# Dense layers of a two-layer graph network, chunk by chunk with nodes on partitions

## What is computed

```python
def block(x):                                  # N = 3125, D = 128, H = 4, C = 32, HID = 512
    conv = transformer_conv(x, src, dst, ...)  # softmax over incoming edges, + x @ Wskip.T + bskip
    out1 = conv @ Wout.T + bout
    out2 = _layer_norm(out1 + x, ln1_w, ln1_b)
    h = jax.nn.relu(out2 @ W1.T + b1)
    out3 = h @ W2.T + b2
    return _layer_norm(out3 + out2, ln2_w, ln2_b)
x = _layernorm(x + block(x))
# second layer: w = mlp(embedding(edge_weight)); rows of x @ W_up gathered by src, multiplied by w
# and the edge's direction, summed by dst, then @ W_out
x = _layernorm(x + edge_conv(x, edge_attr_3, edge_weight, src, dst, ...))
return x
```

## Time and profile before

| | us |
|---|---|
| median of 3 runs (2353.87 to 2362.63) | 2357.6 |
| the profiled execution | 2362.86 |
| its span, first to last instruction | 2361.1 |
| first edge loop and its tail end at | 1124.7 |
| dense layers, to the first gather of the second loop | 1299.7 |
| second edge loop ends at | 2321.7 |

### The profile page before, as it was taken

How to read it: one execution, slowest core, us unless ns; L and a number is a source line. 1 busy time by engine, 2 the same in 40 slices (tenths; PEclk the granted TensorE clock), 3 DMA queues, 4 the chain that set the end, 5 groups by cost and what they waited for, 6 DMA issues and landing times.

```text
span 2361.1 us, 43013 instructions
## 1 busy us (share of the span) xinstructions
PE 1914.8 (81%) x12714; PEld 1563.0 (66%) x12714; DVE 1643.9 (70%) x4394; ACT 1201.3 (51%) x2979; POOL 1563.6 (66%) x1617
## 2 busy tenths in 40 slices
PE   5567767776777677676998999989899898998988
PEld 4567667766677667676637666666667676766666
DVE  4767767777767767678413677777777777777774
ACT  2656556565656556552233454445545455454551
POOL 4777777777777777770000777777777777777770
PEclk8799998999989989989797799999999999999997
DMA  8656556555555555560000222222222222222221
GB/s 262 167 155 169 164 152 167 165 162 164 161 167 166 164 159 164 152 180 14 1 0 27 57 57 57 56 57 56 58 57 57 57 57 56 57 57 56 57 55 35
DMA packets 209005, 240.86 MB, mean 102 GB/s; under 512 B 43003, under 2 KB 166268, under 8 KB 208518
## 3 DMA queue, kind: packets, MB, share of 16 engines
q0 software_dynamic: 64480, 158.57, 25.1%
q1 hardware_dynamic: 144294, 79.55, 11.7%
HBM read 226.01 MB, written 11.94 MB: 101 GB/s over the span
## 4 chain that ended last, share of the span: by engine, by line
POOL 54%; issue 20%; PE 15%; DVE 4%; ACT 3%; DMA 3%; DVEq 0%; SPq 0%; POOLq 0%; ACTq 0%
POOL rows L397 32%; POOL rows L384 22%; PE ps L448 3%; PE ps L439 2%; PE ps L550 2%; DVE acc L912 2%; DMA rows<-kv_tab,src_col 2%; PE ps L430 1%; ACT hots L654 1%; PE ps L541 1%; PE ps L571 1%; PE ps L532 1%; PE ps L566 1%; ACT exb L677 1%; ACT hots L657 1%
## 5 line engine op out<-in xcount | busy, mean ns | idle before, releaser
L397 POOL DMA_INDIRECT rows<-up_tab,src_col x806 | 764.0, 948 | 390.2 <-issue 245.3
L384 POOL DMA_INDIRECT rows<-kv_tab,src_col x806 | 793.8, 985 | 272.8 <-issue 266.8
L620 PE MATMUL ps<-hotT,hots 128*128 128x128 f32 x3232 | 453.1, 298 | 87.2 <-DVE hots L1125 87.0
L620 PEld LDWEIGHTS ps<-hotT,hots 128*128 128x128 f32 x3232 | 412.5, 207 | 122.0 <-DVE hots L1125 114.2
L912 DVE TENSOR_TENSOR acc<-acc,ps 128x256 f32 x808 | 335.9, 416 | 216.9 <-PE ps L448 192.2
L1089 DVE TENSOR_TENSOR acc<-acc,ps 128x256 f32 x808 | 334.4, 414 | 15.0 <-PE ps L620 13.1
L448 PE MATMUL ps<-hots,msg 128*128 128x128 f32 x1616 | 329.1, 287 | 9.8 <-DVE acc L912 7.3
L448 PE MATMUL ps<-hots,exb 128*128 128x128 f32 x1616 | 322.1, 282 | 0.0
L668 ACT COPY hotT<-ps 128x512 f32<-128x512 f32 x202 | 117.8, 583 | 359.6 <-PE ps L430 347.9
L1104 DVE TENSOR_TENSOR hots<-rows,yvec 128x384 f32<-128x384 f32 x202 | 114.1, 565 | 235.8 <-DMA rows<-up_tab,src_col 235.8
L448 PEld LDWEIGHTS ps<-hots,msg 128*128 128x128 f32 x1616 | 260.4, 203 | 13.7 <-issue 7.5
(11 more groups left out here) (142 smaller groups left out, 2518.2 us busy)
## 6 DMA issues: line engine op xcount, KB each, us to landing
qwin<-q_tab SPq DMA_DIRECT2D x808, 64.0 KB
rows<-kv_tab,src_col POOLq DMA_INDIRECT x806, 2.9
rows<-up_tab,src_col POOLq DMA_INDIRECT x806, 2.5
hots<-emb_rows SPq DMA_DIRECT2D x202, 16.0 KB
weights<-r_far SPq DMA_DIRECT2D x25, 128.0 KB, 3.5
emb_rows<-weights SPq DMA_DIRECT2D x25, 128.0 KB
kv_tab<-rows SPq DMA_DIRECT2D x12, 256.0 KB, 2.8
dst_lanes<-in_dst_lanes SPq DMA_DIRECT2D x26, 65.0 KB
```

The costliest lines, as they stand in the source:

```text
L384: nc.gpsimd.indirect_dma_start(kvr[:, q % RING, k, :], None, kv_tab, bass.IndirectOffsetOnAxis(src_col[:, t:t + 1].bitcast(U32), 0)).then_ ...
L397: nc.gpsimd.indirect_dma_start(upr[:, q % RING, k, :], None, up_tab, bass.IndirectOffsetOnAxis(src_col[:, t:t + 1].bitcast(U32), 0)).then_ ...
L620: mm = pe.matmul(ps[:, 4 + 2 * (q % 2) + k // 2, (2 * (k % 2) + m) * P:(2 * (k % 2) + m + 1) * P], left[:, q % 2, k, :], hot2[:, q % 2, k, ...
```

## The change

Stage 3 becomes one loop over the chunks in which each engine's list interleaves steps of chunks j-1, j, j+1 and j+2. Up to the division features stay on partitions; the output projection takes a tile's columns as stationary operand and so gives nodes on partitions (`first_out`, into PSUM bank 2). A node's mean and variance are then taken along the row by DVE (`bn_stats`, `bn_aggr` in `moments_of`); ACT takes the root and applies mean and scale in one pass per tile (`normalise`). `turn1` transposes to features for the hidden layer, where `second_input` applies the first norm's weight and bias; `mlp` gives rows again, with the residual as a product with the identity. `centre` and `third_input` apply the second norm together with x and its bias row; `turn2` transposes the third norm's input ahead of that norm, whose mean is folded into `wup` and whose scale is applied in `up_rows`. The new x is written later by `new_x`.

The skip layer is folded: `wx` = Wskip.T Wout.T + I and the row `const1` = bskip Wout.T + bout. `prepare` makes them in the tail of the first edge loop: a transpose in PE's slot 203 and three products in slot 205; a copy and two scalings on DVE at the end of slot 204 and four 128x128 operations in slot 206. SP loads x by rows (`x_rows`, 1.6 MB) after `msg_ready` 190 and four vectors over all partitions. POOL adds the second norm's bias row to `xb` after the last gather of the first loop and ahead of the memset of `acc`. The final stage has nodes on partitions too, with two buffers `last`, and stores rows of the result. Left out below: the views into SBUF, the semaphores, functions that a sentence above describes, and all removed lines; `kv_in` and `g_in` become one list `rows_in`.

```diff
             batch_rows(BATCHES - 1)
+            sp.wait_ge(msg_ready, 190)
+            sp.dma_start(xb.rearrange("p t f -> p (t f)"), a["x_rows"]).then_inc(ld["dense"], 16)
+            sp.wait_ge(qe_ready, 200)
+            sp.dma_start(qwin[:, 3].rearrange("p t f -> p (t f)"), a["row_vecs"].partition_broadcast(P)).then_inc(ld["dense"], 16)
...
+                sp.wait_ge(fin_ready, j + 1)
+                tiles = chunk_tiles(j)
+                full = [t for t in tiles if (t + 1) * P <= N]
+                if full:
+                    sp.dma_start(out[full[0] * P:(full[-1] + 1) * P, :].rearrange("(t p) f -> p t f", p=P),
+                                 last[:, j % 2, 0:len(full), :]).then_inc(fin_out, 16)
...
+            pool.wait_ge(ld["dense"], 32)
+            nc.gpsimd.tensor_tensor(xb, xb, row_l2b.unsqueeze(1).to_broadcast([P, TABLE_TILES, D]), ALU.add).then_inc(xb_ready, 1)
             pool.wait_ge(conv, NCH)
             nc.gpsimd.memset(acc[:], 0.0).then_inc(acc2_zero, 1)
...
+                if q in (NQ + 1, NQ + 3):
+                    prepare((q - NQ) // 2)
...
+            def first_out(j):
+                pe.wait_ge(conv, j + 1)
+                if j:
+                    pe.wait_ge(u1_sb, j)
+                for k, t in enumerate(chunk_tiles(j)):
+                    to = ps[:, 2, k * P:(k + 1) * P]
+                    pe.matmul(to, xT[:, tile_cols(t)], wx, start=True, stop=False)
+                    mm = pe.matmul(to, convs[:, j % 2, k * P:(k + 1) * P], wt(W_OUT), start=False, stop=True)
+                mm.then_inc(out1_mm, 1)
...
+                    pe.wait_ge(out2_sb, j)
+                for k in range(count(j)):
...
+            def mlp(j, ks):
+                pe.wait_ge(h_sb, 4 * (j + 1))
+                if j:
+                    pe.wait_ge(u2_sb, j)
+                for k in ks:
+                    to = ps[:, 6, k * P:(k + 1) * P]
+                    pe.matmul(to, out2T[:, j % 2, k * P:(k + 1) * P], ident, start=True, stop=False)
+                    for m in range(HID // P):
+                        mm = pe.matmul(to, hiddens[:, j % 2, m, k * P:(k + 1) * P], wt(W_2 + m * P), start=False, stop=(m == HID // P - 1))
+                if ks and ks[-1] == count(j) - 1:
+                    mm.then_inc(mlp_mm, 1)
...
+            denominators(0)
+            inverses(0)
+            denominators(1)
+            first_out(0)
+            turn1(0)
+            for j in range(NCH + 1):
+                ks = list(range(count(j))) if j < NCH else []
+                if j + 1 < NCH:
+                    inverses(j + 1)
                 if j < NCH:
+                    hidden(j, 0)
+                    hidden(j, 1)
+                if j + 1 < NCH:
+                    first_out(j + 1)
+                if j < NCH:
+                    hidden(j, 2)
+                    hidden(j, 3)
+                if j + 2 < NCH:
+                    denominators(j + 2)
+                if j:
+                    turn2(j - 1)
+                if j < NCH:
+                    mlp(j, ks[:2])
+                if j:
+                    up(j - 1)
+                if j < NCH and ks[2:]:
+                    mlp(j, ks[2:])
+                if j + 1 < NCH:
+                    turn1(j + 1)
             pe.wait_ge(up_sb, NCH)
...
+            def root(n, j):
+                act.wait_ge(moment[n], j + 1)
+                nc.scalar.activation(rstd[:, n, j % 2, 0:count(j)], moments[:, n, j % 2, 0:count(j), 1], ACT.Sqrt,
+                                     bias=consts[:, K_EPS:K_EPS + 1]).then_inc(std[n], 1)
+            def normalise(n, j, to, ready):
+                act.wait_ge(shift[n], j + 1)
+                for k in range(count(j)):
+                    op = nc.scalar.activation(to(k), to(k), ACT.Identity, bias=nshift[:, n, j % 2, k:k + 1], scale=rstd[:, n, j % 2, k:k + 1])
+                op.then_inc(ready, 1)
...
+            spread_inverse(1)
+            first_normal(0)
+            for j in range(NCH + 1):
+                if j < NCH:
+                    second_input(j)
+                    relu(j, 0)
+                    relu(j, 1)
+                if j:
+                    root(1, j - 1)
+                if j < NCH:
+                    relu(j, 2)
+                    relu(j, 3)
+                if j >= 2:
+                    new_x(j - 2)
+                if j:
+                    turned2(j - 1)
+                if j + 2 < NCH:
+                    spread_inverse(j + 2)
+                if j + 1 < NCH:
+                    first_normal(j + 1)
+                if j:
+                    root(2, j - 1)
...
+            new_x(NCH - 1)
...
+                    dve.wait_ge(ld["dense"], 32)
+                    v.tensor_tensor(wx, ps[:, 0, P:2 * P], ident, ALU.add).then_inc(prep_sb, 1)
+                    v.tensor_tensor(const1, ps[:, 0, 2 * P:3 * P], row_bout, ALU.add).then_inc(prep_sb, 1)
+                    v.tensor_tensor(wup, wt(W_UP), ps[:, 0, 3 * P:4 * P], ALU.subtract).then_inc(stats[1], 1)
+                    dve.wait_ge(stats[1], 1)
+                    v.tensor_scalar(wup, wup, 1.0 / np.sqrt(32).item(), None, ALU.mult).then_inc(prep_sb, 1)
...
+                if q in (NQ + 2, NQ + 4):
+                    prepare((q - NQ) // 2 - 1)
...
+            def moments_of(n, g, j, src):
+                for k in range(count(j)):
+                    op = v.bn_stats(bst[:, k, :], src[:, k, :])
+                op.then_inc(stats[n], 1)
+                dve.wait_ge(stats[n], g + 1 + (n == 1))
+                for k in range(count(j)):
+                    op = v.bn_aggr(moments[:, n, g % 2, k, :], bst[:, k, :])
+                op.then_inc(moment[n], 1)
...
+                if j:
+                    dve.wait_ge(turn1_mm, j)
+                v.tensor_tensor(u1[:, 0:count(j), :], bank(2, j), wide(const1, j), ALU.add).then_inc(u1_sb, 1)
+                dve.wait_ge(u1_sb, j + 1)
+                moments_of(0, j, j, u1)
...
+                moments_of(1, j, j, u2)
+                dve.wait_ge(moment[1], j + 1)
+                for k in range(count(j)):
+                    op = v.scalar_tensor_tensor(out=u2[:, k, :], in0=u2[:, k, :], scalar=moments[:, 1, j % 2, k, 0:1], in1=row_l2w,
+                                                op0=ALU.subtract, op1=ALU.mult)
+                op.then_inc(za_ready, 1)
...
+                dve.wait_ge(xb_ready, 1)
+                dve.wait_ge(out1_mm, j + 1)
+                for k, t in enumerate(chunk_tiles(j)):
+                    op = v.scalar_tensor_tensor(out=z[:, t, :], in0=u2[:, k, :], scalar=rstd[:, 1, j % 2, k:k + 1], in1=xb[:, t, :],
+                                                op0=ALU.mult, op1=ALU.add)
+                op.then_inc(z_ready, 1)
...
+            def up_rows(j):
+                dve.wait_ge(inv[2], j + 1)
+                dve.wait_ge(up_mm, j + 1)
+                if j >= 2:
+                    dve.wait_ge(up_out[j % 2], 16 * (j // 2))
+                v.tensor_tensor(exb[:, j % 2, 0:count(j), :], bank(7, j),
+                                rstd[:, 2, j % 2, 0:count(j)].unsqueeze(2).to_broadcast([P, count(j), D]), ALU.mult).then_inc(up_sb, 1)
...
+            invert_sums(0)
+            invert_sums(1)
+            divide(0)
+            first_sum(0)
+            inverse_root(0, 0, 0)
+            shifts(0, 0, 0)
+            for j in range(NCH + 1):
+                if j:
+                    second_sum(j - 1)
+                if j + 1 < NCH:
+                    divide(j + 1)
+                if j:
+                    centre(j - 1)
+                    third_input(j - 1)
+                if j + 1 < NCH:
+                    first_sum(j + 1)
+                if j + 2 < NCH:
+                    invert_sums(j + 2)
+                if j + 1 < NCH:
+                    inverse_root(0, j + 1, j + 1)
+                    shifts(0, j + 1, j + 1)
+                if j:
+                    third_moments(j - 1)
+                    inverse_root(2, j - 1, j - 1)
+                    shifts(2, j - 1, j - 1)
+                    up_rows(j - 1)
...
+            def final_sum(j):
                 dve.wait_ge(fin_mm, j + 1)
+                if j >= 2:
+                    dve.wait_ge(fin_out, 16 * (j - 1))
+                v.tensor_tensor(last[:, j % 2, 0:count(j), :], bank(j % 4, j), z[:, CT * j:CT * j + count(j), :], ALU.add).then_inc(fin_sb, 1)
+                dve.wait_ge(fin_sb, j + 1)
+                moments_of(0, NCH + j, j, last[:, j % 2])
+            def final_scale(j):
+                inverse_root(0, NCH + j, j)
+                shifts(0, NCH + j, j)
+            for j in range(NCH + 1):
+                if j < NCH:
+                    final_sum(j)
+                if j:
+                    final_scale(j - 1)
```

376 lines of the change are left out of this document (177 added, 199 removed).

## The result

| | before | changed |
|---|---|---|
| median of four runs, us | 2357.9 | 2304.5 |
| lowest and highest | 2353.9, 2362.6 | 2301.0, 2310.5 |
| profiled execution (span) | 2362.9 (2361.1) | 2303.3 (2301.5) |

The ratio is 0.978, 95% interval 0.976 to 0.980. The forecast was 2303.6 us with a range from 2288 to 2331.

A forecast was written before the change was run, and what follows sets the result against it. Gather-paced edge loops, the second a fixed 1022 us block, with PE-bound dense layers between. 2362.9 + 4.6 (tail) - 60.5 (dense) + 1.9 (end) = 2308.9; less 5.3 for the median: 2303.6 us, range 2288 to 2331.

The forecast's parts named there:

- Tail: End of the first edge loop: DVE's prepare adds 1.6 us and POOL's addition 3, together +4.6 us.
- POOL's term of 3 us: First loop's tail: POOL's bias addition holds up DVE, cost bounded by 0 and 8 us, taken as 3.
- the rule that I weighed: Tail: GpSimd reading SBUF and DVE with two SBUF inputs exclude each other; 7 us lost instead of 3.
- Dense: Dense layers between the edge loops: 114.5 us in place of 175.0, so -60.5 us.
- Round 0: First round of the dense loop: 11.0 us at full and 21 at half clock, taken as 15.5.
- the price of 14.5 us: Dense round's period if the moments (BN_STATS, BN_AGGR) take their longer time, two of them on the path, +1.8 us.
- Epilogue: Dense part after the last full MLP chunk: nearly all DVE work, 7.1 + 3.0 + DMA of 1.5 to 2, 12 us.
- End: Last projection and layer norm: rounds serial through the store's landing, 6.2 us each; 41.3 against 39.4, +1.9 us.
- Handoffs as the bound: Rival 1, dense rounds: handoffs, not PE, set the round at 17 us; total 2327 us; chance 0.27.
- PE at half clock: Rival 2, dense rounds: PE stays at 1.2 GHz, round 24 us; total 2357, no change; chance 0.05.
- The serial chain: Rival 3, dense layers: chunks don't overlap, 35 us each at half clock; total 2408 us, slower; chance 0.03.
- That the kernel does less than it says: Whole change: does less than described, for instance late x_rows loads that would stop prepare; chance 0.02.

The follow-up runs named there:

- The last run: Better version of the changed kernel, denominators back behind the hidden products, last tile of the second MLP product behind the next chunk's turn1: 2275.5 us against 2360.9, ratio 0.963.
- the control run on the other chip: The changed kernel, unaltered, on a chip granting PE a lower clock over the span: 3082.8 us against 3136.7 for the kernel before, ratio 0.982.

## Why the prediction was right, point by point

**The frame** (a fixed second loop behind the dense layers) held: that loop moved by 2.2 us, and the 63.8 us of the dense part arrived in the span.

**Tail, +4.6 foreseen, +3.1 measured.** `prepare` is as foreseen: passes of 0.28 us with 0.2 to 0.3 from start to start, 1.4 us in all, and a wait of 0.3. POOL's term of 3 us came to 3.7. But the two terms were to be the whole, and between last gather and last add the changed kernel has 65.4 us against 58.7, 6.7 more; its last gather came 3.6 us earlier (1062.4 against 1066.0), for which the change gives no reason. So the term was too small by 2 us, and the execution's own spread hid it; that it looks too large in the table is luck. The last run, on a chip as fast, has POOL's addition behind the last add and 61.4 us there: 4.0 less than the changed kernel, near the 3.7 of the long product, and 2.7 more than before, against the 1.6 foreseen for `prepare`. These are single executions, and that run also has eight unread products on PE ahead of the last add.

The choice there was between 0, 3 and 8 us, and the rule that I weighed was right as a mechanism: the Trainium skill (SBUF — State Buffer, section "SBUF: two separate sides") calls the shared port pair "an **exclusive lock**, not a bandwidth split". The seven products of 4.41 to 6.88 us that end about 0.55 us after POOL's instruction agree, and so do the untouched adds L1010 with one input in PSUM. The estimate of POOL's length, 7 us, which the prediction worked out from the 2.6 cycles per element of the Trainium skill (GPSIMD Engine Reference, section 3.1), agrees with the 6.95 of the trace. What I had missed is that the loss depends on when DVE next issues such a product: here 3.1 us after POOL's start.

**Dense, -60.5 foreseen, -63.8 measured.**
- Prologue: the first hidden product came 17.4 us after the last add (18.8 foreseen).
- Round 0 from there to the next turn: 12.1 us against 15.5. This was the term chosen between 11 and 21; PE was back at its full clock within the round, so the choice should have been nearer to the lower end.
- Rounds: 13.43 us, PE's own work (13.3 foreseen). BN_STATS and BN_AGGR, the operation without a row, take 0.87 and 0.38 for four, 1.25 against the 1.3 that I chose between 1.0 and 2.2.
- Waits, 1.1 us per round foreseen: none. PE is busy for 13.40 of 13.40 us, and ACT's normalisation is ready 0.93 us ahead of the turn. The run with more DVE work shows why the feared path was not one: DVE had 2.19 us of idle time in the middle of it. My own schedule left DVE idle from 8.1 to 10.3 us of the round, and the price of 14.5 us added the longer moments to the path as if that gap weren't there. The slack that was really thin stood elsewhere: the handoff over `second_input` had 0.05 us of it, and the prediction, which counted only the path over the normalisation (0.65 us), doesn't price it.
- Epilogue, 12 foreseen, 16.3 measured. Here a term was wrong: I counted it as DVE's work and at the full clock. The rows at the end of the changed kernel's dense part, and the same of the control run on the other chip:

```profile
1227.40 1.12 PE L595 MATMUL ps<-consts,xT 128*128 128x128 f32 x4 [2.12 <-DVE xT L1191]
...
1230.45 1.92 PE L603 MATMUL ps<-qwin,hots 128*128 128x128 f32 x8
1232.46 0.69 DVE L1206 TENSOR_TENSOR exb<-ps,bw 128x512 f32<-128x512 f32 x1 [2.71 <-PE ps L603]
```

```profile
1662.90 0.66 PE L595 MATMUL ps<-consts,xT 128*128 128x128 f32 x4 [2.13 <-DVE xT L1191]
...
1664.51 1.06 PE L603 MATMUL ps<-qwin,hots 128*128 128x128 f32 x8
1665.66 0.69 DVE L1206 TENSOR_TENSOR exb<-ps,bw 128x512 f32<-128x512 f32 x1 [0.76 <-PE ps L603]
```

With PE at half clock DVE waits 2.71 us for the up products, at full clock 0.76; the epilogue takes 16.3 and 14.0 us. So 2.3 us of the miss go with the clock, 1.95 of them in this one wait. The other 2 remain at the full clock, where DVE is busy for 9.2 of the 14.0 us and waits for PE and ACT between its passes; I put them down to handoffs that I had left out, which no run isolates.

The misses cancel in part: -1.4 for the prologue, -3.4 for round 0, -5.5 for the waits, +4.3 for the epilogue. Rounds 1 to 5 took 65.4 us against 62.7 without waits, +2.7, as the one-tile chunk at the end takes off 1.8 us and not 3.8. Together that is the -3.3 by which the dense part beat the forecast.

**End, +1.9 foreseen, +3.3 measured.** The mechanism is as written, DVE waiting for the store with a round of 6.37 us (6.2 foreseen). But the terms of the sum, 36.3 + 2.1 + 2.5, make 40.9 and not 41.3, so the foreseen change was +1.5 and the miss is 1.8 us: 0.2 up to the first landing, 0.6 in four rounds of 6.36 in place of 6.2 (ACT's four passes take 1.65 in place of 1.35 us), 0.6 from the last chunk's sum to its store, and 0.35 in the last store with the close (2.85 in place of 2.5).

**The total.** The median, 2304.5, lies 0.9 us above the forecast, and that closeness is partly luck: the stages of the profiled executions beat the forecast by 5.6 us, with misses of up to 5.5 us in single terms that cancel, and the two executions profiled lie 6 us farther apart than the medians.

**The rivals.** Handoffs as the bound: excluded for the changed kernel by the two runs with less PE and more DVE work. But two handoffs to ACT were covered by PE's work with little to spare, 0.05 us at the hidden product and 0.39 at the MLP product, and they held the round as soon as the work in front of them got shorter. PE at half clock: not in rounds 1 to 5, but in parts of the prologue, round 0 and the epilogue (0.72, 0.82 and 0.62 granted on average). The serial chain: it is what the kernel would be without its order, and the price that I gave, 35 us at half clock, is what the run shows (35.8, at a granted 0.64 to 0.69), where in the expectation of that run I moved to 30 and was wrong. That the kernel does less than it says: no sign of it.

## What to carry to other kernels

When one engine sets the pace of a woven loop, look at what stands between each handoff and its answer before making anything there cheaper: work saved inside a handoff's shadow comes back as a wait of the same length, and saving pays only where something else can fill the hole. Price a chain at the clock that its own gaps will leave it: here the edges of the woven loop were granted 0.62 and 0.72 and its middle 1.00. And one buffer per store costs nothing where memory is free, while with two buffers DVE waited for a store in each round of the end stage, 4.1 of 6.4 us.

## What was unexpected of the hardware

- The same kernel takes 2358 or 3192 us, by the chip: 0.92 or 0.78 of PE's clock over the span. The second edge loop of the kernel before takes 1022 us at a granted 0.94 and 1391 at 0.77, while the changed kernel's rounds 1 to 3 run at 1.00 and take 13.43 us on all of them. Why a chip grants less in the loops no run shows.
- A DVE product of 0.68 us took up to 6.88 us beside one POOL instruction, ten times its length, while adds with one input in PSUM ran on.
- Unread products in PE's gaps went with a granted clock of 0.85 to 1.00 in two runs, but with 0.74 in the prologue of a third. They gained at most 1.8 us, and nothing in the epilogue, where the products that DVE waited for had already run at the full clock.
